# Cross-attention's key and value projections by seven block products each (Strassen), the last keys of all batches in one product, block sums on VectorE

## The reference

```
q = x1 @ Wq.T + bq;  k = x2 @ Wk.T + bk;  v = x2 @ Wv.T + bv     # x1 = layernorm(x), x2 = ctx_1024
attn = softmax(q k^T / sqrt(32)) over 257 keys, 16 heads;  out = (attn v) @ Wo.T + bo
```

## Time and profile before

| | us |
|---|---|
| median of 3 runs | 1935.95 (1934.34 to 1938.89) |
| profiled execution, whole | 1926.86 |
| its span (first to last instruction) | 1925.2 |
| busy: PE, DVE, ACT, POOL | 1844.9, 713.3, 549.1, 188.1 |
| mean granted TensorE clock | 0.977 |

### The profile page before, as it was taken

The page is one execution under the profiler, slowest core; times in us unless marked ns, Lnnn a source line. Parts: engine busy times, 40 slices in busy tenths (PEclk is TensorE's granted clock), DMA queues, the critical chain, the costliest instruction groups (busy, mean ns, idle before and its releaser), DMA issues.

```text
span 1925.2 us, 35009 instructions
## 1 busy us (share of the span) xinstructions
PE 1844.9 (96%) x15118; PEld 917.9 (48%) x15118; DVE 713.3 (37%) x1541; ACT 549.1 (29%) x1178; POOL 188.1 (10%) x156
## 2 busy tenths in 40 slices
PE   5999879999999999999989999999999999999977
PEld 2454553333333233223346566665656566565644
DVE  3777753222222222222224443333334333434422
ACT  1444302222222222222222232333323233232321
POOL 2222240000000000000011100001000000100000
PEclk9999879999999999999999999999999999999988
DMA  9754377999999999999962300001000100100000
GB/s 362 236 187 172 141 298 301 402 404 405 404 409 408 408 406 409 409 408 404 366 229 78 121 23 27 14 23 28 23 18 23 29 12 24 28 23 18 12 1 11
DMA packets 84703, 370.67 MB, mean 193 GB/s; under 512 B 7407, under 2 KB 25327, under 8 KB 51841
## 3 DMA queue, kind: packets, MB, share of 16 engines
q1 hardware_dynamic: 79744, 355.78, 48.1%
q0 software_dynamic: 4864, 13.51, 2.0%
HBM read 353.14 MB, written 16.84 MB: 192 GB/s over the span
## 4 chain that ended last, share of the span: by engine, by line
PE 89%; DVE 3%; issue 3%; ACT 3%; DMA 1%; POOL 1%; POOLq 0%; DVEq 0%; ACTq 0%
PE ps L1416 41%; PE ps L1600 17%; PE ps L1612 17%; PE ps L1831 3%; PE ps L1726 1%; PE ps L1480 1%; ACT arena L723 1%; PE ps L1752 1%; PE ps L1588 1%; PE ps L1464 1%; PE ps L1711 1%; PE ps L1426 1%; PE ps L1801 0%; POOL arena L576 0%; PE ps L1809 0%
## 5 line engine op out<-in xcount | busy, mean ns | idle before, releaser
L1416 PE MATMUL ps<-arena 128*128 128x512 f32 (+3 forms) x3120 | 886.3, 440 | 18.4 <-ACT arena L723 6.5
L1416 PEld LDWEIGHTS ps<-arena 128*128 128x128 f32 x3120 | 526.8, 193 | 345.0 <-issue 278.5
L1612 PE MATMUL ps<-arena 128*32 128x512 f32 x2304 | 341.9, 593 | 0.0
L1614 PE MATMUL ps<-arena 128*32 128x512 f32 x768 | 340.9, 593 | 0.0
L1600 PE MATMUL ps<-arena 128*32 128x512 f32 x3072 | 339.5, 596 | 0.2 <-issue 0.2
L576 POOL TENSOR_TENSOR arena<-arena 128x1 f32<-128x1 f32 (+3 forms) x80 | 134.6, 1683 | 974.0 <-DVE arena L982 499.6
L1600 PEld LDWEIGHTS ps<-arena 128*32 128x32 f32 x3072 | 98.1, 108 | 235.2 <-issue 233.7
L1612 PEld LDWEIGHTS ps<-arena 128*32 128x32 f32 x2304 | 92.7, 109 | 215.5 <-issue 212.9
L1218 DVE STREAM_TRANSPOSE arena<-arena 128x512 f32<-128x512 f32 x96 | 68.4, 713 | 215.9 <-ACT arena L831 215.9
L831 ACT ACTIVATE arena<-ps 128x512 f32<-128x512 f32 x96 | 57.3, 597 | 276.4 <-PE ps L1600 276.4
L1228 DVE TENSOR_TENSOR arena<-ps,arena 80x512 f32<-80x512 f32 x32 | 22.0, 688 | 306.8 <-ACT arena L844 306.8
(11 more groups left out here) (200 smaller groups left out, 1249.1 us busy)
## 6 DMA issues: line engine op xcount, KB each, us to landing
arena<-in_w SPq DMA_DIRECT2D x64, 4096.0 KB, 18.5
arena<-in_ctxT SPq DMA_DIRECT2D x8, 2056.0 KB, 7.8
arena<-in_ctxT SPq DMA_DIRECT2D x32, 514.0 KB, 3.8
arena<-in_ctx SPq DMA_DIRECT2D x8, 2048.0 KB
xe_rows<-arena SPq DMA_DIRECT2D x8, 640.0 KB, 14.3
y_rows<-arena POOLq DMA_DIRECT2D x32, 160.0 KB, 6.4
arena<-xe_rows SPq DMA_DIRECT2D x30, 160.0 KB, 18.8
arena<-in_wqkv0T SPq DMA_DIRECT2D x1, 3072.0 KB, 19.6
```

The costliest lines, as they stand in the source:

```text
L1416: ins = pe.matmul(dst, lhsT, rhs, start=(n == 0), stop=(n == len(pairs) - 1))
L1612: pe.matmul(ps[q4[g], bY(s), :], hT[s][:, g, t, q4[c]], w2_sb[s][:, t * HB + c, :], start=(t == 0 and c == 0), stop=(t == ST - 1 and c == ...
L1614: ins = pe.matmul(ps[q4[ST], bQ(s, t), :], hT[s][:, t, ST, q4[c]], w2_sb[s][:, ST * HB + c, :], start=(c == 0), stop=(c == HB - 1))
```

## The change

Each batch's 256 x 512 context block and each 512 x 512 weight are cut into 2 x 2 blocks. A product of two such matrices is then formed from seven block products instead of eight, with sums of blocks before and after. The weight sums S1 to S4 are made once per matrix on VectorE (S1 in place); the context sums T1 to T4 once per batch, shared by keys and values (T3 in place in the context buffer). A key product is four matmuls of 128 columns, a value product two of 256. The products go to three PSUM banks in turn, and each result block grows in SBUF: ScalarE copies out the first product, VectorE adds the others. Per batch VectorE so has three context sums and T4, two, four and two sums and a tiny copy for the keys, two, three and two sums for the values.

The 257th row's keys (`klast`) are now also one product for all batches, made in the opening together with the last rows' values; a batch's column is copied into place. The last rows of the context are loaded ahead of the expert loop instead of after it; bv comes as one row, not spread over 128 partitions, and enters PV as 16 matmuls of 128 columns. The memset of PTd moves behind the opening's values. ScalarE's four key blocks of 257 become two of 128 and one value block of 256. The interleaving strings stay as they are. Memory regions are rearranged for the sums. The core of the diff (indent cut by eight blanks):

VectorE: the sums of weights and context (line 1273 on), before the last result of the experts:

```diff
+    def weight_sums(A11, A12, S1, A22, S2, S3, S4):
+        TT(S3, A11, S1, ALU.subtract).then_inc(S_rdy, 1)
+        step(TT(S1, S1, A22, ALU.add))
+        step(TT(S2, S1, A11, ALU.subtract))
+        TT(S4, A12, S2, ALU.subtract).then_inc(S_rdy, 1)
+    def context_sums(bb):
+        B11, B12, B21, B22 = keys_of(bb % 2)
+        dve.wait_ge(ctxc_in[bb % 2], 16 * (bb // 2 + 1))
+        wait(dve, v_ps, NP * (bb - 1) + 3)
+        step(TT(T1, B12, B11, ALU.subtract))
+        step(TT(T2, B22, T1, ALU.subtract))
+        TT(B12, B22, B12, ALU.subtract).then_inc(T_rdy, 1)
+    def context_last(bb):
+        B11, B12, B21, B22 = keys_of(bb % 2)
+        wait(dve, v_ps, NP * (bb - 1) + 6)
+        TT(T4, B21, T2, ALU.subtract).then_inc(T_rdy, 1)
+    dve.wait_ge(wK_in, 16 * WK)
+    weight_sums(A11k, A12k, S1k, A22k, S2k, S3k, S4k)
+    TT(dbk, bk_sb[:, KH:KD], bk_sb[:, 0:KH], ALU.subtract)
+    context_sums(0)
     result_out(E - 1, 1, E // 2 - 1)
     dve.wait_ge(y_ps, ST * E)
-    step(dve.memset(one.PTd, 0.0))
-    dve.memset(vlast_c, 0.0).then_inc(dve_set, 1)
-    step(dve.memset(zero_c[0:1, :], 0.0))
+    context_last(0)
+    dve.memset(vlast_c[0:32], 0.0).then_inc(dve_set, 1)
     step(dve.reduce_sum(same_b[0:NL, :], id_sb[0:NL, 0:NL].rearrange("p (q b) -> p b q", q=HQ), AX.X))
```

VectorE: the sums of the products, and the opening:

```diff
+    def keys_first(bb):
+        dve.wait_ge(k_act, K_ACT * bb + KH)
+        dve.wait_ge(k_ps, NP * bb + 2)
+        TT(kC12, half(kY), kC11, ALU.add).then_inc(k_dve, 1)
+        dve.wait_ge(k_ps, NP * bb + 4)
+        TT(kC11, half(kX), kC11, ALU.add).then_inc(k_dve, 1)
+    def keys_second(bb):
+        dve.wait_ge(k_ps, NP * bb + 5)
+        dve.wait_ge(k_dve, K_DVE * bb + 1)
+        for m in range(KH):
+            STT(kC21[:, m, :], ps[:, kY, m * P:(m + 1) * P], dbk[:, m:m + 1], kC12[:, m, :],
+                ALU.add, ALU.add).then_inc(k_dve, 1)
+        dve.wait_ge(k_dve, K_DVE * bb + 4)
+        TT(kC22, half(kZ), kC21, ALU.add).then_inc(k_dve, 1)
+        TT(kC12, half(kZ), kC12, ALU.add).then_inc(k_dve, 1)
+    def keys_third(bb):
+        dve.wait_ge(k_ps, NP * bb + 6)
+        TT(kC21, half(kX), kC21, ALU.add).then_inc(k_dve, 1)
+        dve.tensor_copy(kT_c[:, :, 2 * P:S], klast[:, :, bb:bb + 1]).then_inc(k_dve, 1)
+        dve.wait_ge(k_ps, NP * bb + 7)
+        dve.wait_ge(k_dve, K_DVE * bb + 6)
+        TT(kC12, half(kZ), kC12, ALU.add).then_inc(k_dve, 1)
+    def values_first(bb):
+        dve.wait_ge(v_act, bb + 1)
+        dve.wait_ge(v_ps, NP * bb + 2)
+        TT(vC12, ps[:, vY, 0:HF], vC11, ALU.add).then_inc(v_dve, 1)
+        dve.wait_ge(v_ps, NP * bb + 4)
+        TT(vC11, ps[:, vX, 0:HF], vC11, ALU.add).then_inc(v_dve, 1)
+    def values_second(bb):
+        dve.wait_ge(v_ps, NP * bb + 5)
+        dve.wait_ge(v_dve, V_DVE * bb + 1)
+        TT(vC21, ps[:, vY, 0:HF], vC12, ALU.add).then_inc(v_dve, 1)
+        dve.wait_ge(v_dve, V_DVE * bb + 3)
+        TT(vC22, ps[:, vZ, 0:HF], vC21, ALU.add).then_inc(v_dve, 1)
+        TT(vC12, ps[:, vZ, 0:HF], vC12, ALU.add).then_inc(v_dve, 1)
+    def values_third(bb):
+        dve.wait_ge(v_ps, NP * bb + 6)
+        TT(vC21, ps[:, vX, 0:HF], vC21, ALU.add).then_inc(v_dve, 1)
+        dve.wait_ge(v_ps, NP * bb + 7)
+        dve.wait_ge(v_dve, V_DVE * bb + 5)
+        TT(vC12, ps[:, vZ, 0:HF], vC12, ALU.add).then_inc(v_dve, 1)
+    dve.wait_ge(clT_rdy, 1)
+    TT(dT, clastT[:, KH:KD, :], clastT[:, 0:KH, :], ALU.subtract).then_inc(lasts_dve, 1)
+    dve.wait_ge(wV_in, 16 * WV)
+    keys_first(0)
+    weight_sums(A11v, A12v, S1v, A22v, S2v, S3v, S4v)
+    keys_second(0)
+    dve.wait_ge(lasts_ps, 2)
+    step(TT(klast, ps[:, 5, KD * B:2 * KD * B].rearrange("p (m b) -> p m b", m=KD),
+            bc(bk_sb.unsqueeze(2), P, KD, B), ALU.add))
+    keys_third(0)
+    dve.wait_ge(lasts_ps, 3)
+    dve.tensor_copy(vlast_all[0:B, :], ps[0:B, 7, :]).then_inc(lasts_dve, 1)
+    for stage in (values_first, values_second, values_third):
+        stage(0)
+    step(dve.memset(one.PTd, 0.0))
```

VectorE: the pieces 2 to 7 of a batch in `cross`:

```diff
+            following = b < NB - 1 or more
+            if bb > 0:
+                values_first(bb)
+            if b == NB - 1 and more:
+                queries()
+            yield
+            if bb > 0:
+                values_second(bb)
+            if following:
+                context_sums(bb + 1)
+            yield
+            if bb > 0:
+                values_third(bb)
+            if following:
+                context_last(bb + 1)
...
-            yield
-            yield
-            yield
+            for stage in (keys_first, keys_second, keys_third):
+                if following:
+                    stage(bb + 1)
+                yield
```

TensorE: the products:

```diff
+    def key_product(bank, Sb, Tb):
+        for m in range(KH):
+            group(ps[:, bank, chunk(m)], [(Sb[:, k, chunk(m)], Tb[:, k, :]) for k in range(KH)],
+                  k_ps if m == KH - 1 else None)
+    def value_product(bank, Tb, Sb):
+        group(ps[:, bank, 0:HF], [(Tb[:, k, :], Sb[:, k, :]) for k in range(KH)], v_ps)
+    def keys_first(bb):
+        B11, T3, B21, B22 = keys_of(bb % 2)
+        pe.wait_ge(ctxc_in[bb % 2], 16 * (bb // 2 + 1))
+        if bb > 0:
+            pe.wait_ge(pt_ev, 2 * (bb - 1) + 1)
+            if bb % NB == 0:
+                pe.wait_ge(lastX_rdy, bb // NB)
+        key_product(kX, A11k, B11)
+        if bb > 0:
+            pe.wait_ge(v_dve, V_DVE * (bb - 1) + 6)
+        pe.wait_ge(T_rdy, 2 * bb + 1)
+        key_product(kY, S2k, T2)
+        if bb > 0:
+            pe.wait_ge(v_dve, V_DVE * bb)
+        key_product(kZ, S1k, T1)
+        pe.wait_ge(k_act, K_ACT * bb + KH)
+        key_product(kX, A12k, B21)
+    def keys_second(bb):
+        B11, T3, B21, B22 = keys_of(bb % 2)
+        pe.wait_ge(k_dve, K_DVE * bb + 1)
+        key_product(kY, S3k, T3)
+    def keys_third(bb):
+        B11, T3, B21, B22 = keys_of(bb % 2)
+        pe.wait_ge(T_rdy, 2 * bb + 2)
+        pe.wait_ge(k_dve, K_DVE * bb + 2)
+        key_product(kX, A22k, T4)
+        pe.wait_ge(k_dve, K_DVE * bb + 6)
+        key_product(kZ, S4k, B22)
+    def values_first(bb):
+        B11, T3, B21, B22 = keys_of(bb % 2)
+        if bb > 0:
+            pe.wait_ge(exp_c, HG * bb + 1)
+        else:
+            pe.wait_ge(k_dve, 4)
+        value_product(vX, B11, A11v)
+        if bb > 0:
+            pe.wait_ge(exp_c, HG * bb + 2)
+        value_product(vY, T2, S2v)
+        if bb > 0:
+            pe.wait_ge(exp_c, HG * bb + 3)
+        else:
+            pe.wait_ge(k_dve, K_DVE)
+        value_product(vZ, T1, S1v)
+        pe.wait_ge(v_act, bb + 1)
+        value_product(vX, B21, A12v)
```

TensorE: `cross` after the scores:

```diff
+            if b == 0:
+                pe.wait_ge(clast_in, 32)
+                for g in range(HG):
                     for q in range(HQ):
+                        pe.matmul(ps[q4[q], bPV, chunk(g)], bv_row[:, g, q4[q]], ones_sb[32:33, :],
+                                  start=(g == 0), stop=False)
+            if bb > 0:
+                values_first(bb)
+            yield
             for j in range(2):
+                if bb > 0:
+                    (values_second, values_third)[j](bb)
+                if j == 0:
+                    pe.wait_ge(pn_rdy, (HG + 1) * bb + (HG + 1))
+                else:
+                    pe.wait_ge(v_dve, V_DVE * bb + 3)
                 for q in range(HQ):
                     ins = pe.transpose(ps[:, bT(j), chunk(q)], P_c[:, q, j * P:(j + 1) * P], id_sb)
                 ins.then_inc(pt_ps, 1)
+                if j == 1 and b == NB - 1:
+                    pe.wait_ge(pt_ev, 2 * bb + 1)
+                    pe.transpose(ps[0:NL, bLast, 0:P], last_p.rearrange("p q b -> p (q b)"), id_sb
+                                 ).then_inc(last_ps, 1)
+                yield
+            if following:
+                keys_first(bb + 1)
             yield
+            for half in range(2):
+                if following:
+                    (keys_second, keys_third)[half](bb + 1)
+                if half == 0:
+                    pe.wait_ge(pt_ev, 2 * bb + 2)
+                    pe.wait_ge(v_dve, V_DVE * bb + V_DVE)
+                    if b == 0:
+                        pe.wait_ge(vlast_in, 16 * HQ * (i + 1))
+                for g in range(2 * half, 2 * half + 2):
+                    if g == HG - 1 and following:
+                        pe.wait_ge(k_dve, K_DVE * bb + 2 * K_DVE)
+                        if b == NB - 1:
+                            pe.wait_ge(Qbd_rdy, i + 2)
+                    for j in range(2):
+                        for q in range(HQ):
+                            h = HQ * g + q
+                            pe.matmul(ps[q4[q], bPV, g * P + b * T:g * P + (b + 1) * T],
+                                      v_c[:, j, h * DH:(h + 1) * DH],
+                                      PT_c[:, j, q * P + g * T:q * P + (g + 1) * T],
+                                      start=False, stop=False)
+                if half == 0:
+                    yield
             if b == NB - 1:
                 if not more:
```

(74 more changed lines are left out.)

163 lines of the change are left out of this document (86 added, 77 removed).

## The result

The changed kernel takes 2055.35 us (median of four runs, 2049.51 to 2057.28), the kernel before 1937.42 in runs beside it: ratio 1.0604, 95% interval 1.0576 to 1.0633, 6% slower. The forecast was 2068 us (2000 to 2115). The profiled execution's span is 2055.5 us, 130.3 above the one before.

| stretch | before, us | after, us | difference | forecast |
|---|---|---|---|---|
| start to the end of the experts | 975.1 | 980.1 | +4.9 | 0 |
| opening, to the first scores | 25.5 | 43.9 | +18.4 | +13 |
| first tile | 74.6 | 88.5 | +13.9 | +7 |
| six tiles | 669.4 | 754.3 | +84.9 | +101 |
| last tile and tail | 180.6 | 188.8 | +8.2 | +11 |

A forecast was written before the change was run, and what follows sets the result against it. TensorE's matmul time bounds the last phase; waits of 17.4 less gains of 5.6 plus clock 5 give +16.8 us a tile. Six tiles 101, +13, +7, +11 make +132 on 1926.9: 2059, median 2068 us, range 2000 to 2115.

The forecast's parts named there:

- The places of the waits: TensorE waits for VectorE's sums at five places of each batch, and for ScalarE's copy: 17.4 us a steady tile.
- The gain of 5.6 us a tile: Steady tile: cheaper key and value products save 5.1 us, two vanished waits for ScalarE's copy another 0.5.
- one sum 0.42: VectorE: each sum of 256 elements taken as 0.42 us, between a low end of 0.35 and a high of 0.69.
- rival 4: Products not cheaper, weight loads bind at 0.28 us: about +8 more, 2076 us; inside the forecast's chance of 0.50.
- The clock: Steady tile: four waits of 1.9 to 2.75 us bring half clock, 1.8 each; 5 us a tile taken.
- rival 1: Clock stays full, as the skill warns only of idle gaps longer than any listed: +96, 2032 us; chance 0.28.
- The waits would not feed on themselves: Against rival 3, lateness feeding on itself with a third of a tile at half clock: +32 a tile, 2160 us; chance 0.12.
- Opening: Before the last phase, VectorE's weight sums, key and value sums, klast and memset delay the first add to near 1003: +13.
- First tile: No tail, but the adds of gathered rows stand before value and key sums: +7 us.
- Last tile: First three batches without the next layer norm, fourth without keys: +8, clock +3, together +11 us.
- The sum: Six steady tiles x 16.8 = 101, +13, +7, +11: +132 us on the profiled execution's 1926.9 us.
- offset of 9 us for the median: Median of the runs taken as 9 us above the profiled execution, turning 2059 into 2068 us.

The follow-up runs named there:

- e6: Changed kernel's instructions in another order on VectorE and ScalarE, TensorE's wait for the last key sum moved ahead of the scores; 1961.29 us, ratio 1.0129.
- e5: Changed kernel with six products of 128 rows and 128 columns filling each of TensorE's three waits of 2.1 us; 2040.78 us, ratio 1.0561.
- e2: Changed kernel with three products of zeros (32 rows, 256 columns) in each of TensorE's three waits of 2.1 us; 2051.49 us, ratio 1.0624.
- e4: Changed kernel with VectorE's order altered in the opening alone, and TensorE's wait for the values' weight sums moved before the last values; 2041.64 us, ratio 1.0571.
- e7: Changed kernel with the reorderings of e6 and e4 together; 1947.95 us, ratio 1.0084 to the kernel before.
- e8: Values by seven products as in the changed kernel, keys as in the kernel before, orders of e4 and e6 where they apply; 1928.6 us, ratio 0.9977.
- e10: e8 with VectorE's first-tile sums and adds and third-batch group sums reordered, and first-batch keys beginning in another bank; 1919.28 us, ratio 0.9921.

## Why the prediction was right, step by step

- **The places of the waits: right, all too long.** Forecast 17.4 us a tile, shown 12.1. Seven long ones came out 8 to 24% shorter (2.08 for 2.75 and 2.7, 2.15 for 2.5, 1.58 for 1.9, 1.10 for 1.2, 1.05 for 1.3, 0.74 for 0.95), the others by half or more (0.26 for 0.8, four times 0.25 for 0.5 to 1.1); the wait of 0.25 for the seventh value product isn't in the rows. Part of it is the step "one sum 0.42": independent sums follow each other after 0.33 us (1376.31 to 1376.64), though each lasts 0.41; VectorE's 65.96 us instead of the forecast 69 fit that.
- **The gain of 5.6 us a tile: too high.** A key product takes 0.93 us (forecast 0.94; 20 of them, 4.71 us for five), the first value products 0.89 (0.88); rival 4 is out. But at full clock, in e6, TensorE is busy 108.27 us of a tile, against 111.52 before: 3.25 us less, where the forecast had 5.1 from cheaper products. Its other 0.5, the two waits for ScalarE's copy, did go. Some 0.7 us of the difference sit between products, where the rows name no wait: in three of the four batches the sixth and seventh value products take 2.0 us together (1378.19 to 1380.19 in batch 1) where two take 1.76. Where the rest is stays open.
- **The clock: 5 us a tile forecast, about 4 measured.** e5, which keeps TensorE at work, is 3.3 us a tile faster than the changed kernel on the mean and 4.0 in a tile whose clock stays at 1.00. Near in size, wrong in the rule I used (a gap of 1.8 us costs 1.8): of the four waits that it counted, only those of batches 3 and 4 did it, in each of the six tiles; behind batch 1's 2.08 us the clock stayed full in five of the six, behind batch 2's 1.58 in all. On rival 1's rule (the Trainium skill, TensorE: Matmul & The Clock Gate, HAM oscillation) the trace has decided: no gap of the tile is longer than 2.15 us, and the granted clock was 0.50 behind one. The next section of that page of the Trainium skill (A second HAM failure mode: psum-queue depth-cycling) tells of a kernel in which short, frequent idles between groups of products made the clock go down and up; this case agrees as far as short idles go, with half clock behind gaps of 2.15 us and, in e2, of 0.69.
- **The waits would not feed on themselves:** right. Five of the six tiles take 125.96 to 126.71 us, the first of them 123.2.
- **Opening: +13 forecast, +18.4 measured.** The wait for the weight sums (3, measured 2.70) was priced, the half clock behind it wasn't: 0.50 at 992 to 996 us. It and the late layer norm, which came out later than forecast (the add before it ran at 1011.45 us, forecast near 1003; 5 of the difference are the later end of the experts), are what e4 took back, 13.2 us.
- **First tile: +7 forecast, +13.9 measured.** I priced the adds as waits of value sums; the late layer norm for the second tile and the last-rows sums hold key products too (3.04 us in the second batch, 1.97 in the fourth), and the clock falls there as well. In e2 and e5, with the same code there, the first tile takes 85.5 and 85.6 us, so some 3 of the 13.9 come and go between executions.
- **Last tile: +8.2 for +11.**
- **The sum: +130 for +132, in part by luck.** Opening and first tile were 12 us too low, the six tiles and the last 19 too high, and 4.9 of the 130 aren't the change's. In a tile, waits too long and a gain too high cancelled in part likewise. The offset of 9 us for the median didn't come back: the profiled execution is the slowest of the four runs (2057.28 us), 1.9 above their median, and so most of the 13 us between 2068 and 2055 is that offset.
- **Two readings that don't hold.** TensorE's "near 108" busy in a tile of 129 us doesn't follow from the prediction's own terms: 129 less 17.4 of waits is 111.5; measured were 113.94 of 126.02. And from Wo's result to the value block shows 5.2 us, not 5.3.

## What to carry to other kernels

When fewer multiplications are bought with sums on another engine, the room that engine has on average says nothing: ask at each product which sum it needs, and what stands ahead of that sum in that engine's fixed order. Cut the pieces ahead of it where they wait for a third engine, and sort before judging the change: here the same instructions were 6.0% slower than the kernel before in one order and 0.8% (e7) in another. Apply the idea first where the saving per product is large against a sum: the value half gained, the key half, with half the saving and as many sums, didn't in the orders tried (a steady tile takes 111.5 us in e7 and 110.5 in e8). With the first tile put in order too, as e10 has it for the values alone, the key half wasn't measured; whether it could break even there is open.

## What the runs showed of the hardware

TensorE's clock fell to 0.50 behind waits of 2.08 and 2.15 us in which the engine stood still. Behind the same wait of 2.08 us it stayed full in one batch and fell in another, with other work around it. With 1.53 us of a wait filled by 32-row products and 0.69 us idle it still fell in one place (batch 4 in e2), and with 0.63 us idle it stayed full in another (batch 3). With 128-row products and 0.81 us idle it stayed at 1.00 at the end of four tiles and fell at two (e5).

VectorE started a sum 0.33 us behind an independent one, though each lasts 0.41 us.
